# Writing rounded rows as float16 numbers of 2^-24 steps instead of int16 with a cast behind

## The reference, cut to what matters

```python
def _act_quant(x):                       # one scale for each row
    scale = 127.0 / clip(max(abs(x), axis=-1), EPS)
    return round(clip(x * scale, -128.0, 127.0)) / scale
def _weight_quant(w):                    # -1, 0 or 1, one scale for the matrix
    scale = 1.0 / clip(mean(abs(w)), EPS)
    return round(clip(w * scale, -1.0, 1.0)) / scale
def _bitlinear(x, w):
    return einsum('bsi,oi->bso', _act_quant(_rmsnorm(x)), _weight_quant(w))

x = x + xattn(ctx, _layernorm(x))        # 4 batches, 512 rows of 512; a top-30% threshold per row
gate, up = silu(_bitlinear(n, w_gate)), _bitlinear(n, w_up)      # n = _layernorm(x), 512 -> 2048
x = x + _bitlinear(gate * up, w_down)                            # 2048 -> 512
```

## Time and profile before

| | |
|---|---|
| median of 3 runs | 268.02 us (267.92 to 268.54) |
| the profiled execution | 268.02 us, of which the span of instructions is 266.2 us |
| busy: PE, DVE, ACT, POOL | 216.5, 214.1, 194.6, 169.0 us |
| matmuls | 962 |
| transposing DMAs issued by SP | 53 |

### The profile page before, as it was taken

One profiled execution on the slowest core, in us unless ns is written; L12 is line 12 of the kernel. 1 busy time (PEld: TensorE's weight loads), 2 busy tenths in 40 slices (PEclk: granted clock), 3 DMA queues, 4 the chain that ended last, 5 costly groups with the idle time before them and its releaser, 6 DMA issues.

```text
span 266.2 us, 3714 instructions
## 1 busy us (share of the span) xinstructions
PE 216.5 (81%) x962; PEld 107.3 (40%) x974; DVE 214.1 (80%) x376; ACT 194.6 (73%) x333; POOL 169.0 (63%) x322
## 2 busy tenths in 40 slices
PE   7704620225998877999999999999999999999995
PEld 7301300222744432443445444434454444444434
DVE  0585987976869999898899999998898959367881
ACT  2499999899999999996949999736349443654030
POOL 2045787786988646678978878873886812505620
PEclk9965595555799999999999999999999999999999
DMA  4999999999655499420801382330714505743656
GB/s 128 394 374 360 360 230 397 242 317 214 182 113 86 79 178 159 80 59 1 140 1 28 52 139 61 79 68 19 194 37 101 102 0 100 173 133 71 119 101 216
DMA packets 79143, 39.19 MB, mean 147 GB/s; under 512 B 67984, under 2 KB 70544, under 8 KB 78608
## 3 DMA queue, kind: packets, MB, share of 16 engines
q1 hardware_dynamic: 79120, 38.94, 58.9%
HBM read 17.96 MB, written 4.19 MB: 83 GB/s over the span
## 4 chain that ended last, share of the span: by engine, by line
PE 30%; POOL 13%; POOLq 13%; DVE 11%; ACT 10%; issue 9%; DMA 6%; DVEq 4%; SPq 2%; ACTq 0%
PE U L405 9%; PE G L391 9%; PE DN L424 9%; DMA C<-in_ctx 5%; ACT junk_c L514 3%; POOLq L986 3%; ACT WuT L556 2%; POOL S L1047 2%; POOL qx L1016 2%; POOL X L982 2%; ACT S L563 2%; POOLq L948 2%; DVE S L764 2%; POOL sig L939 2%; POOLq L958 2%
## 5 line engine op out<-in xcount | busy, mean ns | idle before, releaser
L391 PE MATMUL G<-WgT,xqT 128*128 128x512 bf16 x256 | 60.5, 379 | 3.6 <-ACT sg L539 3.2
L539 ACT ACTIVATE sg<-G,gsc 128x1024 f32<-128x1024 f32 x32 | 35.5, 1110 | 37.2 <-PE G L391 34.8
L405 PE MATMUL U<-WuT,xqT 128*128 128x512 bf16 x256 | 60.5, 379 | 1.6 <-DVE S L764 1.6
L514 ACT ACTIVATE junk_c<-rows,srch 128x512 int8<-128x512 f32 (+1 forms) x76 | 53.8, 713 | 1.9 <-POOL srch L961 1.2
L764 DVE TENSOR_TENSOR S<-U,sg 128x1024 f32<-128x1024 f32 x31 | 37.9, 1222 | 13.0 <-PE U L405 7.7
L424 PE MATMUL DN<-WdT,S 128*128 128x512 bf16 x197 | 45.5, 379 | 0.9 <-DMA S<-S 0.3
L1047 POOL TENSOR_SCALAR S<-S,qh 128x2048 int16<-128x2048 f32 x15 | 30.0, 2002 | 25.1 <-DVE qh L829 24.9
L391 PEld LDWEIGHTS G<-WgT,xqT 128*128 128x128 bf16 x256 | 24.6, 98 | 35.1 <-issue 3.8
L547 ACT ACTIVATE junk_h<-S 128x2048 int8<-128x2048 f32 x16 | 30.5, 1905 | 10.2 <-DVE S L779 8.6
L405 PEld LDWEIGHTS U<-WuT,xqT 128*128 128x128 bf16 x256 | 24.8, 98 | 32.6 <-DVE S L764 4.3
L769 DVE TENSOR_REDUCE amh<-S 128x1 f32<-128x2048 f32 x15 | 34.1, 2271 | 0.1
(11 more groups left out here) (148 smaller groups left out, 370.4 us busy)
## 6 DMA issues: line engine op xcount, KB each, us to landing
S<-in_L_ffn_w_gate SPq DMA_DIRECT2D x4, 1024.0 KB, 9.2
S<-in_L_ffn_w_up SPq DMA_DIRECT2D x4, 1024.0 KB, 11.9
X<-in_x SPq DMA_DIRECT2D x4, 1024.0 KB, 10.8
S<-in_L_ffn_w_down SPq DMA_DIRECT2D x4, 1024.0 KB, 6.9
out<-X SPq DMA_DIRECT2D x15, 256.0 KB, 2.9
C<-in_ctx SPq DMA_DIRECT2D x2, 256.0 KB, 8.6
C<-in_ctx SPq DMA_DIRECT2D x1, 512.0 KB, 11.5
S<-S SPq DMA_TRANSPOSE x17, 4.3
```

What stands on the lines that cost most here:

```text
L391: last = nc.tensor.matmul(G[:, c * 512:(c + 1) * 512], xqT[:, t, k, :], WgT[:, 4 * n:4 * n + 4, k, :], start=(k == 0), stop=(k == KD - 1))
L405: last = nc.tensor.matmul(U[:, c * 512:(c + 1) * 512], xqT[:, t, k, :], WuT[:, 4 * n:4 * n + 4, k, :], start=(k == 0), stop=(k == KD - 1))
L514: A(junk_c[:, j, :].bitcast(U8) if r == ROUNDS else junk_c[:, j, :], ROWS[a % 2][:, j, :], ACT.Sign, bias=nthr[:, j:j + 1], accum_out=cs[: ...
L539: A(sg[:, u % 2, :], G[:, :], ACT.Silu, scale=gsc[:, b % 2, t:t + 1]).then_inc(silu_done, 1)
```

## The change

The types of the weights and of the rounded rows go from bf16 to float16. The one scaling pass over a row multiplies by 2^-24 too and writes float16. Numbers of that size are below float16's normal range, where its step is 2^-24, so the write itself rounds to whole steps. The factor is taken back in the scales (`gsc`, `usc`, `sud`). The casts `x_cast` and `h_cast`, and those in `last_round`, are gone, with their waits; `qx_ready` and `hq_ready` are now signalled by POOL's pass. The rest of DVE's list stays in its order, and the lists of PE, ACT, POOL and SP are the same as before.

```diff
+UNIT = 2.0 ** -24
...
-        WgT = sb("WgT", [P, F // P, KD, P], BF16)
+        WgT = sb("WgT", [P, F // P, KD, P], F16)
...
-                        act.wait_ge(xi_ready, NT * (a - 1))
+                        act.wait_ge(qx_ready, NT * (a - 1))
...
-            def x_cast(a, *js):
-                c = slice(js[0], js[-1] + 1)
-                dve.wait_ge(xi_ready, NT * a + js[-1] + 1)
-                V.tensor_copy(qx[:, c, :], qx[:, c, :].bitcast(I16)).then_inc(qx_ready, len(js))
...
-                V.tensor_scalar(hq[:, i % 2, f].bitcast(I16), h[:, i % 2, f], qh[:, i % 4:i % 4 + 1], 1.0,
-                                ALU.mult, ALU.mult)
-                dve.drain()
-                V.tensor_copy(hq[:, i % 2, f], hq[:, i % 2, f].bitcast(I16)).then_inc(hq_last, 1)
+                V.tensor_scalar(hq[:, i % 2, f], h[:, i % 2, f], qh[:, i % 4:i % 4 + 1], UNIT,
+                                ALU.mult, ALU.mult).then_inc(hq_last, 1)
...
-            def h_cast(i):
-                dve.wait_ge(hi_ready, i + 1)
-                V.tensor_copy(hq[:, i % 2, :], hq[:, i % 2, :].bitcast(I16)).then_inc(hq_ready, 1)
...
-                    G_.tensor_scalar(qx[:, j, :].bitcast(I16), ROWS[a % 2][:, j, :], qsx[:, j:j + 1], -1.0,
-                                     ALU.mult, ALU.mult).then_inc(xi_ready, 1)
+                    G_.tensor_scalar(qx[:, j, :], ROWS[a % 2][:, j, :], qsx[:, j:j + 1], -UNIT,
+                                     ALU.mult, ALU.mult).then_inc(qx_ready, 1)
...
-                G_.tensor_scalar(hq[:, i % 2, :].bitcast(I16), h[:, i % 2, :], qh[:, i % 4:i % 4 + 1], 1.0,
-                                 ALU.mult, ALU.mult).then_inc(hi_ready, 1)
+                G_.tensor_scalar(hq[:, i % 2, :], h[:, i % 2, :], qh[:, i % 4:i % 4 + 1], UNIT,
+                                 ALU.mult, ALU.mult).then_inc(hq_ready, 1)
```

More of the change, by code:

```diff
@@ L14 @@
 F32 = mybir.dt.float32
-BF16 = mybir.dt.bfloat16
+F16 = mybir.dt.float16
 I32 = mybir.dt.int32
@@ L884, in _ @@
[L884 to L888, removed]
@@ L889, in _ @@
-            sim_stats(2, 0, 1); x1(1, 0); w_quant(2, 0); mul(1); sim_stats(2, 2, 3); h_absmax(0); x1(1, 1)
-            w_quant(2, 1); h_floor(0); h_scale(0); mul(2); x1(1, 2); w_quant(2, 2); w_quant(2, 3); x1(1, 3)
-            h_cast(0); x_absmax(1, 0); mul(3); x_absmax(1, 1); h_absmax(1); h_scale(1); x_stats(2, 0, 1); mul(4)
-            h_cast(1); x_stats(2, 2, 3); x_absmax(1, 2); x_absmax(1, 3); mul(5); x_scale(1, 0, 1, 2, 3)
-            h_absmax(2); h_scale(2); mul(6); x_cast(1, 0, 1); x_cast(1, 2, 3); rank(2, 0); rank(2, 1); rank(2, 2)
@@ L899, in _ @@
-            x_absmax(2, 1); x_absmax(2, 2); x_absmax(2, 3); x_scale(2, 0, 1, 2, 3); mul(14); rank(3, 0)
-            h_scale(6); final(4); x_cast(2, 0, 1); x_cast(2, 2, 3); rank(3, 1); mul(15); rank(3, 2); h_absmax(7)
-            h_scale(7); mul(16); h_cast(6); rank(3, 3); mul(17); final(5); note_misses(3); h_absmax(8); mul(18)
-            h_cast(7); threshold(3); general_path(3); mul(19); h_floor(2); masked(3, 0); final(6); masked(3, 1)
-            masked(3, 2); h_scale(8); h_absmax(9); masked(3, 3); mul(20); final(7); h_cast(8); x1(3, 0); x1(3, 1)
@@ L904, in _ @@
-            h_scale(9); mul(21); x1(3, 2); x1(3, 3); x_absmax(3, 0); x_absmax(3, 1); x_absmax(3, 2); h_cast(9)
-            x_absmax(3, 3); x_scale(3, 0, 1, 2, 3); mul(22); x_cast(3, 0, 1); final(8); h_absmax(10); h_scale(10)
-            mul(23); mul(24); h_absmax(11); h_cast(10); x_cast(3, 2, 3); mul(25); h_scale(11); h_absmax(12)
-            h_floor(3); mul(26); final(9); h_cast(11); h_scale(12); mul(27); mul(28); h_absmax(13); h_cast(12)
-            final(10); mul(29); h_scale(13); h_absmax(14); h_scale(14); final(11); h_cast(13); h_cast(14); mul(30); last_floor()
@@ L909, in _ @@
[L909 to L910 removed]
+            w_abs(0, 0); sim_stats(0, 0, 1); sim_stats(0, 2, 3); w_abs(0, 2); w_abs(0, 3); w_scale(0); w_quant(0, 0)
+            x_stats(0, 0, 1); x_stats(0, 2, 3); w_quant(0, 1); rank(0, 0); rank(0, 1); rank(0, 2); w_scale(1)
+            rank(0, 3); sim_stats(1, 0, 1); sim_stats(1, 2, 3); note_misses(0); threshold(0); general_path(0)
@@ new lines, in _ @@
+            masked(0, 0); masked(0, 1); masked(0, 2); w_quant(0, 2); w_quant(0, 3); masked(0, 3); x_stats(1, 0, 1)
+            x_stats(1, 2, 3); x1(0, 0); x1(0, 1); w_quant(1, 0); x1(0, 2); x1(0, 3); x_absmax(0, 0); x_scale(0, 0)
+            x_absmax(0, 1); x_scale(0, 1); w_quant(1, 1); x_absmax(0, 2); x_scale(0, 2); x_absmax(0, 3)
+            x_scale(0, 3); rank(1, 0); rank(1, 1); rank(1, 2); rank(1, 3); w_quant(1, 2); w_quant(1, 3)
+            note_misses(1); threshold(1); general_path(1); masked(1, 0); masked(1, 1); masked(1, 2); w_scale(2)
@@ new lines, in _ @@
+            masked(1, 3); mul(0); sim_stats(2, 0, 1); x1(1, 0); w_quant(2, 0); mul(1); sim_stats(2, 2, 3)
+            h_absmax(0); x1(1, 1); w_quant(2, 1); h_floor(0); h_scale(0); mul(2); x1(1, 2); w_quant(2, 2)
+            w_quant(2, 3); x1(1, 3); x_absmax(1, 0); mul(3); x_absmax(1, 1); h_absmax(1); h_scale(1)
+            x_stats(2, 0, 1); mul(4); x_stats(2, 2, 3); x_absmax(1, 2); x_absmax(1, 3); mul(5)
+            x_scale(1, 0, 1, 2, 3); h_absmax(2); h_scale(2); mul(6); rank(2, 0); rank(2, 1); rank(2, 2); rank(2, 3)
@@ new lines, in _ @@
+            note_misses(2); mul(7); threshold(2); sim_stats(3, 0, 1); final(0); h_absmax(3); h_scale(3); mul(8)
+            general_path(2); masked(2, 0); masked(2, 1); sim_stats(3, 2, 3); mul(9); final(1); masked(2, 2)
+            masked(2, 3); mul(10); h_absmax(4); h_floor(1); mul(11); x1(2, 0); x1(2, 1); h_scale(4); h_absmax(5)
+            h_scale(5); x_stats(3, 0, 1); x1(2, 2); mul(12); x1(2, 3); final(2); mul(13); x_stats(3, 2, 3); final(3)
+            h_absmax(6); x_absmax(2, 0); x_absmax(2, 1); x_absmax(2, 2); x_absmax(2, 3); x_scale(2, 0, 1, 2, 3)
@@ new lines, in _ @@
+            mul(14); rank(3, 0); h_scale(6); final(4); rank(3, 1); mul(15); rank(3, 2); h_absmax(7); h_scale(7)
+            mul(16); rank(3, 3); mul(17); final(5); note_misses(3); h_absmax(8); mul(18); threshold(3)
+            general_path(3); mul(19); h_floor(2); masked(3, 0); final(6); masked(3, 1); masked(3, 2); h_scale(8)
+            h_absmax(9); masked(3, 3); mul(20); final(7); x1(3, 0); x1(3, 1); h_scale(9); mul(21); x1(3, 2)
+            x1(3, 3); x_absmax(3, 0); x_absmax(3, 1); x_absmax(3, 2); x_absmax(3, 3); x_scale(3, 0, 1, 2, 3)
```

39 lines of the change are left out of this document (15 added, 24 removed).

## The result

The changed kernel takes 267.57 us (median of 15 runs), the kernel before on the same chip 268.56 us (15 runs). The ratio is 0.9969, with a 95% interval from 0.9961 to 0.9977: 0.31% faster, 0.83 us by the ratio. Two of the 15 runs of the changed kernel took 792.28 and 291.3 us; why isn't known, and the ratio leaves them out. The interval reaches from 0.23% to 0.39%, so it doesn't decide between the prediction's classes "faster by over 0.3%" and "within 0.3%". Forecast were 266.9 us and -1.15 us. The profiled execution took 267.45 us with a span of 265.7 us; before it was 268.02 us with 266.2 us.

A forecast was written before the change was run, and what follows sets the result against it. ACT was taken to bound until 119 us, PE until down(13), then the last tile's serial tail. Terms 0 - 0.54 - 0.61 = -1.15 us took 268.02 to 266.9 us, range 265.0 to 268.0 us.

The forecast's parts named there:

- faster by over 0.3%: Outcome class for the whole kernel: a time below 267.2 us, given a chance of 0.60.
- within 0.3%: Outcome class for the whole kernel: a difference under 0.8 us, not told from no change, given a chance of 0.29.
- front, up to gate(8): Casts before 119 us: taken as 0, since ACT and PE are released no later by a cast than by ACT.
- hole at up(17): PE's wait for DVE's mul(16) near 175.3 us: closes wholly once casts from 119 to 175 us go, -0.54 us.
- tail: Last tile: without its casts the second transpose is issued at 257.00 us, when SP is free, not 257.61: -0.61 us.
- the forecast's term for the body: Casts from 119 to 175 us: removing them closes PE's hole at up(17), -0.54 us.
- Types and writes: float16 in matmuls, weights, transposes and in POOL's and DVE's stores costs the same as before: 0.
- the cover: ACT's work hiding the casts before 119 us; without it the pair at 79.70 us is worth 0.41 us at most.
- What is late next is PE itself: At up(17): up(16) lands at 173.7 us, so mul(16) can end at 174.9, ahead of 175.27 us.
- three signs of being wrong: silu(0) moves, gate(8) starts earlier than 118.5 us, or a new wait appears in PE's full stretches.
- only the tail gains: Rival, chance 0.16: the hole at 175.3 us stays because mul(16) stays late for another reason; -0.61 us, 267.4 us.
- Casts from 176 to 250 us: h_cast(6) to h_cast(14) and x_cast(3): taken as 0, since PE is full and has no wait on a transposed row.

The follow-up runs named there:

- all_casts: Changed kernel with POOL and DVE writing int16 again and a DVE pass in place of every cast, leaving only the float16 types: 268.17 us, ratio to before 0.9996.
- tail_only: As all_casts, but with the two passes of last_round as in the changed kernel: 267.70 us, ratio to before 0.9982.
- xcast0b: Changed kernel with int16 writes and a DVE pass behind put back for x of batch 0 alone: 267.80 us, ratio to before 0.9979.
- before_pool_late: The kernel before, without the change, with POOL's h_round(7) put behind the three lnx passes: 269.02 us, ratio to before 1.0023.
- pool_late: Changed kernel with POOL's h_round(7) put behind three short lnx passes, DVE's list untouched: 266.83 us, ratio to before 0.9954.
- rank_mul: Changed kernel with DVE's mul(17) ahead of rank(3, 3) and mul(18) ahead of h_absmax(8): 266.97 us, ratio to before 0.9959.
- pool_split: Changed kernel with POOL's h_round(7) cut into two instructions of 1024 columns: 266.99 us, ratio to before 0.9945.
- body_only: Changed kernel with the two casts of the last tile put back: 268.32 us, ratio to before 0.9995.
- tail_gap: Changed kernel with a needless DVE MAX8 of 0.29 us between the two last scaling passes: 267.73 us, ratio to before 0.9972.

## Why the prediction was right, and where it was not

The measured time lies within the stated range, 265.0 to 268.0 us, but 0.7 us above the forecast. The size of the whole was overstated: -1.15 us forecast, -0.57 us between the two profiled executions, 0.35 to 1 us between medians. The chances that were added up for "faster by over 0.3%" give 0.61, not 0.60, which changes nothing. Step by step, between the profiled executions:

| step | forecast | traced |
|---|---|---|
| front, up to gate(8) | 0 | -0.35 (0.11 of it there before any cast) |
| hole at up(17) | -0.54 | -0.54 |
| new hole at up(18) | none | +0.76 |
| PE from there to the last up | 0 | 0 |
| tail | -0.61 | -0.46 |
| sum | -1.15 | -0.59 |

That the sum stayed negative by as much as this is in part luck: the forecast's term for the body came out at +0.22 us instead of -0.54, and the front, for which it had nothing, brought 0.35 us.

**Types and writes: right.** all_casts (0.9996) and the rows of POOL and DVE show them at 0. By the Trainium skill, "GPSIMD: programming the Q7 cores", section SBUF Data Layout, every converted element goes through the same converter; the trace's 692 ns in either type agrees.

**The front: nearly right.** The forecast was 0, with 0.41 us as a bound if the cover were gone. `gate(8)` came at 118.55 us instead of 118.90. The table of distances splits this. 0.16 us is real: without casts the way from silu(1) to the weight rounding is 1.47 or 1.48 us in eight traces, and 1.63 or 1.64 in four with them, because `w_scale(2)` comes sooner. The cover was ACT's work, which did not reach quite so far. The other 0.18 us is the start of silu(0). 0.11 us of it is there at 55 us already, before the first cast, and is scatter. The other 0.07 us is the first cast of batch 0, which held a short instruction of POOL on the way to `x_coef(0)`. From the timelines, before:

```profile
65.68 0.29 DVE L704 CAST qx<-qx 128x512 bf16<-128x512 int16 x1 [0.82 <-POOL qx L1016]
65.77 0.26 POOL L957 TENSOR_SCALAR srch<-srch 128x2 f32<-128x2 f32 x1
```

and after:

```profile
65.65 0.19 POOL L942 TENSOR_SCALAR srch<-srch 128x2 f32<-128x2 f32 x1
```

The five traces of the table with these casts (before, all_casts, tail_only, xcast0b, before_pool_late) have 0.25 to 0.28 us there, and the traces without them 0.19 us. From the rounding on, `gate(8)` follows at 36.53 us, as before (36.54): ACT is rigid there, as forecast.

**The hole: the mechanism held, its neighbour was missed.** `up(17)` starts back to back: `mul(16)` starts 1.06 us earlier, as soon as PE's `up(16)` lets it, and ends 0.24 us ahead of need. What failed is the step "The hole closes wholly: -0.54 us", with "What is late next is PE itself": it took the next wait of PE for none, and the traces show one of 0.76 us at `up(18)`. I asked only what `mul(16)` waits for. I did not put the next instructions of DVE's list, the rank and `mul(17)`, at their new times beside POOL's list at its own. Both moved up, by different amounts (DVE's rank by 1.66 us, POOL's pass by 1.93 us), and that turned their order round: DVE 0.11 us ahead before, 0.16 us behind after. The row that warned of it was there: POOL's pass in before took 2.42 us at 176.38 us instead of 1.97, beside a rank that was first. pool_late, rank_mul and pool_split, three edits that share nothing but the place, each take the new hole away and give 0.7 to 0.9 us. body_only shows the net of both holes, too little to measure. Of its three signs of being wrong, "a new wait" in PE's full stretches came true, and in this step it was wrong; silu(0) moved by 0.18 us, and `gate(8)` at 118.55 us stayed just short of the third. The rival "only the tail gains" named a shift of DVE's work against POOL, but thought that it would keep the old hole; that its 267.4 us meets the 267.45 us profiled is chance, since the old hole did close and another opened.

**Casts from 176 to 250 us: right from up(19) on.** From there to the last up group it is 65.63 us in both kernels, with the seven casts of h in it gone.

**The tail: right in what binds, 0.15 us too large.** SP's issue sets the second transpose (tail_gap). The term was the issue's busy time of 1.25 us, but from SP's first issue to the start of the second transfer it is 1.33 us (255.65 to 256.98), and the transfer took 3.17 instead of 3.11 us. These two make the difference of 5.28 and 5.13 us.

**What stays open.** Why the kernel before has two groups of times is made likely by one trace, not shown. With the change on the chip where it stood at its upper group the ratio is 0.9969, and 0.9985 on the other.

**The best version** is pool_late: 266.83 us, 0.9954 of the kernel before and 0.88 us below the changed kernel. It ends where the prediction had put the change itself, 266.9 us, though the front and the tail in it are not those of the forecast. rank_mul, at 266.97 us on the same chip, and pool_split, at 266.99 us on another, can't be told from it.

## What to carry to other kernels

Work taken off an engine that isn't the bound pays only at the seams, where the bound waits for that engine, and in the serial tail; find these first and price only them. Then follow both lists past the seam: everything behind the removed work moves up, and each DVE instruction of the kinds that POOL holds (two inputs in SBUF, or a scaling or casting pass over one) must be set against the long POOL pass that it will now run beside. If they meet, split POOL's pass, or exchange it with short ones, and time it, for the exchange that gave 0.88 us here cost 0.6 us in the kernel before.
